# Vision tower on one core: the embedding in two halves, the selection ahead of the logits, and the last layers with new lags

## What is computed

```python
h = _L0_tok_ref(x, L0_tok_W, L0_tok_b)                   # patches 16x16 -> 256 features
h = _layernorm(h + _L0_attn_ref(h, ...))                 # 16 heads, q and k normed
h = _layernorm(h + _L0_ffn_ref(h, ...))                  # 8 experts, top 2, rms norm
h = _layernorm(h + _L1_attn_ref(h, ...))                 # delta rule, a scan over tokens
h = _layernorm(h + _L1_ffn_ref(h, ...))                  # receptance and key, relu squared
h = _layernorm(h + _L2_attn_ref(h, ...))                 # causal attention
h = _layernorm(h + _L2_ffn_ref(h, ...))                  # mixture of 64 small experts by argmax in groups of 16 tokens
h = _layernorm(h + _L3_attn_ref(h, ...))                 # s = lam*s + (1-lam)*x over the tokens
h = _layernorm(h + _L3_ffn_ref(h, ...))                  # int8 product with one scale for all tokens
```

```python
lam = sigmoid(x @ W + b)                                 # _L3_attn_ref
u_gated = (1.0 - lam) * x
s = lam_t * s + ug_t                                     # scan over the tokens of an image
x_int8 = clip(round(x2 / x_scale), -128, 127)            # _L3_ffn_ref, x_scale = max|x2| / 127
out = (x_int8 @ weight_int8.T) * x_scale * weight_scale.T + bias
```

## Time and profile before

| | us |
|---|---|
| median of 3 runs | 1481.62 (1480.22 to 1492.69) |
| profiled execution | 1482.68 |
| its span, first to last instruction | 1481.0 |
| PE busy | 1168.3 (79%) |
| DVE busy | 843.6 (57%) |
| ACT busy | 572.1 (39%) |
| POOL busy | 553.3 (37%) |

### The profile page before, as it was taken

The page is one execution under the profiler, slowest core; times in us unless marked ns, Lnnn a source line. Parts: engine busy times, 40 slices in busy tenths (PEclk is TensorE's granted clock), DMA queues, the critical chain, the costliest instruction groups (busy, mean ns, idle before and its releaser), DMA issues. The chain is left out here.

```text
span 1481.0 us, 23865 instructions
## 1 busy us (share of the span) xinstructions
PE 1168.3 (79%) x8627; PEld 853.3 (58%) x8627; DVE 843.6 (57%) x2014; ACT 572.1 (39%) x1356; POOL 553.3 (37%) x620
## 2 busy tenths in 40 slices
PE   4888886598999999676767777774899998686756
PEld 3666664487988989532334444342777776464432
DVE  2566565511212122556999999994577776324776
ACT  1444442111111211154566666661344444233436
POOL 0111111232332323333899999991112111011336
PEclk9999996699999999898898999995999999776565
DMA  3111100688888887386000000002000040055301
GB/s 128 32 38 44 44 9 15 231 331 334 306 314 303 320 304 265 103 214 163 0 0 1 1 1 1 1 1 78 8 12 8 12 172 2 1 214 183 113 15 58
DMA packets 83300, 162.18 MB, mean 110 GB/s; under 512 B 44080, under 2 KB 62128, under 8 KB 77168
## 3 DMA queue, kind: packets, MB, share of 16 engines
q1 hardware_dynamic: 55488, 111.23, 21.7%
q0 software_dynamic: 10512, 45.10, 8.3%
q10 hardware_dynamic: 17184, 4.33, 1.3%
HBM read 134.28 MB, written 26.35 MB: 108 GB/s over the span
## 5 line engine op out<-in xcount | busy, mean ns | idle before, releaser
L1398 PE MATMUL banks<-made,ident 128*128 128x512 f32 x256 | 152.4, 681 | 90.8 <-DVE made L1609 90.3
L895 PE MATMUL banks<-rowsT,w_up 128*128 128x128 f32 x1716 | 202.2, 278 | 0.1
L895 PEld LDWEIGHTS banks<-rowsT,w_up 128*128 128x128 f32 x1716 | 198.9, 195 | 0.7 <-DMA w_up<-in_up_w 0.4
L1661 POOL TENSOR_TENSOR ys<-xT_d,q_by_time 128x1024 f32<-128x1024 f32 x63 | 148.7, 2361 | 19.3 <-ACT xT_d L1481 9.8
L1504 ACT ACTIVATE banks<-banks,rate 128x256 f32<-128x256 f32 x256 | 104.1, 445 | 116.4 <-DVE made L1600 116.4
L1398 PEld LDWEIGHTS banks<-made,ident 128*128 128x128 f32 x256 | 41.7, 203 | 154.7 <-ACT banks L1504 129.9
L1665 POOL TENSOR_TENSOR ys<-ys 128x512 f32<-128x512 f32 x126 | 124.8, 990 | 9.9
L910 PE MATMUL banks<-w_down,hT 128*128 128x256 f32 x468 | 115.1, 388 | 0.6 <-DVE res L1079 0.6
L1069 DVE TENSOR_TENSOR hT<-banks,silu 64x128 f32<-64x128 f32 x39 | 11.0, 283 | 173.0 <-ACT silu L953 173.0
L839 POOL DMA_DIRECT2D w_down<-in_down_w x39 | 22.8, 584 | 197.6 <-PE banks L910 192.5
L910 PEld LDWEIGHTS banks<-w_down,hT 128*128 128x128 f32 x468 | 82.6, 189 | 22.0 <-issue 13.9
(11 more groups left out here) (315 smaller groups left out, 2388.4 us busy)
## 6 DMA issues: line engine op xcount, KB each, us to landing
w_up<-in_up_w SPq DMA_DIRECT2D x39, 1408.0 KB, 5.9
w_down<-in_down_w POOLq DMA_DIRECT2D x39, 768.0 KB, 4.9
inter<-res_x SPq DMA_DIRECT2D x16, 512.0 KB, 2.6
back<-inter SPq DMA_DIRECT2D x16, 512.0 KB, 3.7
patches<-in_patches SPq DMA_DIRECT2D x16, 384.0 KB, 3.1
f<-in_f SPq DMA_DIRECT2D x6, 1024.0 KB, 10.6
ys<-token_rows SPq DMA_DIRECT2D x16, 256.0 KB, 2.8
xn_rows<-xn_all SPq DMA_DIRECT2D x16, 128.0 KB, 1.7
```

The costliest lines, as they stand in the source:

```text
L895: ins = pe.matmul(out[:, m * P:(m + 1) * P], w[:, c, m * P:(m + 1) * P], x[:, c, :], start=(c == 0), stop=(c == 1))
L1398: pe.matmul(S[(t + 1) % 2][:, halves[h], :, :], ident[:, :], outer[:, halves[h], :, :], start=False, stop=True, skip_group_check=True).the ...
L1661: pool.tensor_tensor(qs[:, :, :, :], Sc[(t + 1) % 2][:, :, :, :], bcast(qt[:, t, :, :], 2, HD), ALU.mult).then_inc(sem("qs_made"), 1)
```

## The change

Embedding. `embed` is split: PE does `second_half(t)` at the start of a tick and `first_half(t+1)` after `values(t)`; `first_half(0)` comes before the loop. `turn_xn` moves on PE from behind `values` to behind `scores`, and waits for hT_copied too; `copy_xnT` moves on ACT from behind `copy_v` to behind `copy_hT`.

Middle layers. `select` (lag 5) comes ahead of `logit` (lag 4).

Last layers. mote_bias and own are loaded ahead of f1 and f2 on semaphores of their own; ACT and POOL wait for those alone at their start. The first tile's back is loaded in four pieces, two of them (12 of 16 quads) ahead of the last store. The scan is written with steps of x: y holds x(t-1) - x(t), made by POOL (`steps_of_x`), and state = (y + state) * lam gives s - x, so DVE adds 2x. xT, lam and y have a zero column ahead of each image in place of the memset. y is turned with four matmuls of 64 columns of weights each. All lags of the stage change. In the integer stage the clamp at -128 is gone (DVE writes qb in bf16 itself), the third norm goes from ACT (with POOL's shift) to POOL, `turn_v` has lag 2 and `int_sums` and `dequantize` lag 1; DVE's list (quantize lag 0, add_int lag 2) is as before.

```diff
-        def embed(t):
+        def embed(t, chunks):
+            for c in chunks:
+                ins = pe.matmul(X, patches[t % SLOTS_IN][:, c, :], w_tok[:, c, :], start=(c == 0),
+                                stop=(c == PC - 1), skip_group_check=True)
+            return ins
+
+        def first_half(t):
             pe.wait_ge(sem(f"patches{t % SLOTS_IN}"), 16 * (t // SLOTS_IN) + 16)
             if t >= 4:
                 pe.wait_ge(sem("xnT_copied"), t - 3)
-            for c in range(PC):
-                ins = pe.matmul(X, patches[t % SLOTS_IN][:, c, :], w_tok[:, c, :], start=(c == 0),
-                                stop=(c == PC - 1))
-            ins.then_inc(sem("embedded"), 1)
+            embed(t, range(0, PC // 2))
+
+        def next_half(t):
+            if t + 1 < T:
+                first_half(t + 1)
+
+        def second_half(t):
+            embed(t, range(PC // 2, PC)).then_inc(sem("embedded"), 1)
...
         def turn_xn(t):
             pe.wait_ge(sem("xn_made"), t + 1)
+            pe.wait_ge(sem("hT_copied"), min(t + 4, T))
             transposes(pe, halves(XNT), xn_all[:, t, :], ident[:, :], DC).then_inc(sem("xnT_made"), 1)
...
-        ticks([(0, embed), (2, turn_out), (0, turn_h), (2, project), (1, scores), (0, queries_keys), (0, values),
-               (3, turn_xn), (1, turn_p), (0, turn_qk), (3, route_scores), (1, attend)])
+        first_half(0)
+        ticks([(0, second_half), (2, turn_out), (0, turn_h), (2, project), (1, scores), (3, turn_xn),
+               (0, queries_keys), (0, values), (0, next_half), (1, turn_p), (0, turn_qk), (3, route_scores),
+               (1, attend)])
...
-        ticks([(2, copy_oT), (0, copy_hT), (0, squares), (1, exponent), (0, head_guess), (0, copy_v), (3, copy_xnT),
+        ticks([(2, copy_oT), (0, copy_hT), (3, copy_xnT), (0, squares), (1, exponent), (0, head_guess), (0, copy_v),
                (1, copy_PT), (0, copy_qk), (2, rms)])
...
         ticks([(1, turn_x1), (3, scores), (0, delta_out), (2, turn_x2), (1, receptance_key), (4, turn_x3),
-               (4, logit), (5, select), (3, turn_p), (1, key_value), (3, attend), (4, turn_perm),
+               (5, select), (4, logit), (3, turn_p), (1, key_value), (3, attend), (4, turn_perm),
...
-weights = [(mote_bias, "mote_bias"), (own, "own_tok"), (w_lam, "lam_w"), (b_lam, "lam_b"), (w8, "int8_w"),
-           (w_scale, "int8_scale"), (bias, "int8_b")]
+weights = [(w_lam, "lam_w"), (b_lam, "lam_b"), (w8, "int8_w"), (w_scale, "int8_scale"), (bias, "int8_b")]
+SPLIT = 12
...
+        sp.dma_start(mote_bias[:], io["mote_bias"]).then_inc(sem("mote_bias"), 16)
+        sp.dma_start(own[:], io["own_tok"]).then_inc(sem("own"), 16)
...
+        def first_back(quads):
+            for p in range(3):
+                sp.wait_ge(sem(f"stored{p}"), 16 * len(range(p, quads.stop, 3)))
+            at = slice(4 * quads.start, 4 * quads.stop)
+            for g in range(2):
+                sp.dma_start(back[0][g * ME + at.start:g * ME + at.stop, :, :], inter[0:GPT, at, :]
+                             .rearrange("(k g) e d -> g e k d", g=2)[g]).then_inc(sem("back0"), 16)
+
         for q in range(QUADS):
             sp.wait_ge(sem("res_low"), q + 1)
             sp.wait_ge(sem("res_high"), q + 1)
             sp.dma_start(inter[:, 4 * q:4 * q + 4, :], res[q % 3][:, :, :]).then_inc(sem(f"stored{q % 3}"), 16)
-        for p in range(3):
-            sp.wait_ge(sem(f"stored{p}"), 16 * len(range(p, QUADS, 3)))
-        for t in range(T):
+            if q == QUADS - 2:
+                first_back(range(0, SPLIT))
+        first_back(range(SPLIT, QUADS))
+        for t in range(1, T):
...
-            pe.wait_ge(sem(f"back{t % BACKS}"), 16 * (t // BACKS) + 16)
+            pe.wait_ge(sem(f"back{t % BACKS}"), 16 * (t // BACKS) + (64 if t % BACKS == 0 else 16))
...
-            transposes(pe, halves(scanned_bank(t)), y[t % 2], ident[:, :], DC).then_inc(sem("y_turned"), 1)
+            for c in range(DC):
+                for i in range(2):
+                    ins = pe.matmul(scanned_bank(t)[i * TOK:(i + 1) * TOK, c * P:(c + 1) * P],
+                                    y[t % 2][:, c, i, 1:TOK + 1], ident[:, :], start=True, stop=True,
+                                    skip_group_check=True)
+            ins.then_inc(sem("y_turned"), 1)
...
-        mix_back(0)
-        ticks([(2, turn_y), (0, turn_x), (0, one_ahead(mix_back)), (0, lam_logits)], 2)
+        ticks([(0, mix_back), (4, turn_y), (2, lam_logits), (1, turn_x)], 4)
         pe.wait_ge(sem("row_top"), 1)
         pe.transpose(banks[:, 2, 0:P], top[:, 0:1].to_broadcast([P, P]), ident[:, :]).then_inc(sem("tops"), 1)
         pe.wait_ge(sem("w_ready"), 1)
-        ticks([(0, turn_q), (1, turn_v), (0, int_sums)], 1)
+        ticks([(0, turn_q), (2, turn_v), (1, int_sums)], 2)
...
         def copy_xT(t):
             act.wait_ge(sem("xT_made"), t + 1)
             if t >= 2:
-                act.wait_ge(sem("ug"), t - 1)
-            act.copy(flat(xT[t % 2]), turned_bank(t)).then_inc(sem("xT_copied"), 1)
+                act.wait_ge(sem("stepped"), t - 1)
+                act.wait_ge(sem("lam_logits"), t - 1)
+            act.copy(segments(xT[t % 2])[:, :, 1:TOK + 1], spread(turned_bank(t))).then_inc(sem("xT_copied"), 1)
...
-        def third_norm(t):
-            if t >= 2:
-                act.wait_ge(sem(f"out{t % 2}"), 16 * (t // 2))
-            normed(3, res_q[t % 2][:, :], r3, t)
-
-        act.wait_ge(sem("weights"), 16 * len(weights))
+        act.wait_ge(sem("mote_bias"), 16)
...
+        act.wait_ge(sem("weights"), 16 * len(weights))
         act.copy(w[:, :, :], w8[:, :, :].bitcast(I8)).then_inc(sem("w_ready"), 1)
-        ticks([(0, first_norm), (0, copy_xT), (2, second_norm), (0, gate)], 2)
+        ticks([(1, first_norm), (2, gate), (1, copy_xT), (5, second_norm)], 5)
         act.wait_ge(sem("scaled"), 1)
-        ticks([(0, copy_qT), (0, dequantize), (2, third_norm)], 2)
+        ticks([(0, copy_qT), (1, dequantize)], 1)
...
+        def steps_of_x(t):
+            pool.wait_ge(sem("xT_copied"), t + 1)
             if t >= 2:
...
-        pool.wait_ge(sem("weights"), 16 * len(weights))
+                pool.wait_ge(sem("y_turned"), t - 1)
+            x_now = segments(xT[t % 2])
+            pool.tensor_tensor(segments(y[t % 2])[:, :, 1:TOK + 1], x_now[:, :, 0:TOK], x_now[:, :, 1:TOK + 1],
+                               ALU.subtract).then_inc(sem("stepped"), 1)
+
+        def third_norm(t):
+            root(3, t)
+            if t >= 2:
+                pool.wait_ge(sem(f"out{t % 2}"), 16 * (t // 2))
+            pool.tensor_scalar(res_q[t % 2][:, :], r3[t % 2][:, :], agg[3][t % 2][:, 0:1],
+                               agg[3][t % 2][:, 1:2], ALU.subtract, ALU.mult).then_inc(sem("ln3_done"), 1)
+
+        for b in (*xT, *lam, *y):
+            pool.memset(segments(b)[:, :, 0], 0.0).then_inc(sem("padded"), 1)
+        pool.wait_ge(sem("padded"), 6)
+        pool.wait_ge(sem("own"), 16)
         for t in range(T):
             pool.tensor_tensor(perm_t[:, t, :], perm_t[:, t, :], own[:, :], ALU.mult).then_inc(sem("owned"), 1)
-        ticks([(0, rstd(1)), (2, rstd(2))], 2)
-        ticks([(0, clamp), (2, rstd(3))], 2)
+        ticks([(0, rstd(1)), (1, steps_of_x), (4, rstd(2))], 4)
+        ticks([(0, third_norm)], 0)
 
...
-            dve.tensor_tensor(r2[t % 2][:, :], x[t % 4][:, :], scanned_bank(t), ALU.subtract
-                              ).then_inc(sem("added2"), 1)
+            dve.scalar_tensor_tensor(out=r2[t % 2][:, :], in0=x[t % 4][:, :], scalar=2.0, in1=scanned_bank(t),
+                                     op0=ALU.mult, op1=ALU.add).then_inc(sem("added2"), 1)
...
         def scan(t):
             dve.wait_ge(sem("lam"), t + 1)
-            dve.wait_ge(sem("xT_copied"), t + 1)
-            dve.scalar_tensor_tensor(out=flat(ug), in0=flat(lam[t % 2]), scalar=1.0, in1=flat(xT[t % 2]),
-                                     op0=ALU.subtract, op1=ALU.mult).then_inc(sem("ug"), 1)
-            dve.wait_ge(sem("ug"), t + 1)
-            dve.memset(flat(lam[t % 2]).rearrange("p (i t) -> p i t", t=TOK)[:, :, 0], 0.0
-                       ).then_inc(sem("cut"), 1)
-            dve.wait_ge(sem("cut"), t + 1)
-            if t >= 2:
-                dve.wait_ge(sem("y_turned"), t - 1)
-            dve.tensor_tensor_scan(y[t % 2][:, :], flat(lam[t % 2]), flat(ug), 0.0, ALU.mult, ALU.add
-                                   ).then_inc(sem("scanned"), 1)
+            dve.wait_ge(sem("stepped"), t + 1)
+            if t < 2:
+                dve.wait_ge(sem("padded"), 6)
+            line = y[t % 2][:, :, :, :].rearrange("p c i t -> p (c i t)")
+            dve.tensor_tensor_scan(line, line, lam[t % 2][:, :, :, :].rearrange("p c i t -> p (c i t)"), 0.0,
+                                   ALU.add, ALU.mult).then_inc(sem("scanned"), 1)
...
         def quantize(t):
             if t >= 2:
-                dve.wait_ge(sem("q_ready"), t - 1)
```

(7 more changed lines are left out.)

39 lines of the change are left out of this document (20 added, 19 removed).

## The result

| | before | after |
|---|---|---|
| median, us | 1480.92 | 1436.38 (1432.96 to 1438.29) |
| profiled execution, us | 1482.68 | 1434.60 |
| its span, us | 1481.0 | 1433.0 |
| mean granted clock of TensorE | 0.896 | 0.911 |

The ratio is 0.968, with an interval of 0.9635 to 0.9726: a gain of 41 to 54 us, 44.5 by the medians. The forecast said 36.6 (1481.6 to 1445) and a range down to 1436. The direction was right, and the gain is larger than forecast. 1436.38 lies at the very edge of the range; by the ratio, which sets aside that the kernel before was 0.7 us faster in these runs than in the forecast's, it is 0.968 x 1481.62 = 1434.2, outside it.

What follows compares the result with a forecast made beforehand. No single engine was taken as the bound; each stage was read by its steady tick. Terms 15.5 + 2.6 + 6.5 + 1.0 + 18.2 - 6.0 = 37.8 us off 1482.7 gave 1444.9, said as 1445; range 1436 to 1460.

Steps and rivals of the forecast that it cites:

- The scan stage: Last layers' scans: less VectorE work and new lags cut the tick from 4.87 to 3.65 us; 18.2 us gained, bounds 12.2 to 20.5.
- The embedding: Embedding with first attention: half an embedding fills a TensorE stop, tick 1.0 us shorter over fifteen tiles; 15.5 us gained.
- The middle layers: Selection ahead of logits: 4.6 us gained over twelve ticks, a loss at the tail; net 2.6 us, bounds -2 and 4.6.
- The experts: Last layers' experts: early mote_bias and own remove TensorE's 6.07 us stop, 6.5 us; first way back loaded partly early, 1.0 us.
- The integer stage: Last layers' integer product: VectorE waits behind its quantizing for both turns, tick 2.79 us against 2.26; 6.0 us lost.
- (a): Scan stage: GpSimd's step of x and VectorE's scan collide on the SBUF ports, 9.9 us less gain, 1455; chance 0.10.
- (b): Scan stage hardly gains, since some wait holds the old 4.87 us tick: 1463; chance 0.07.
- (c): Embedding: TensorE's stop only moves elsewhere: 1461; chance 0.06.
- (e): Scan stage: GpSimd's wait for the turn of y closes an 8.3 us loop each tick, slower than before: 1515; chance 0.03.
- (d): Integer stage does not stall, TensorE finishing both turns before VectorE: 2.5 us gained instead of 6.0 lost, 1436; chance 0.12.

Runs made afterwards that it cites:

- a variant with TensorE busy 66% of the time: The changed kernel with the scan stage's old lags, GpSimd's steps of x and the scan on them kept: 1454.95 us, the stage 75.6 us.

## Why the forecast was off, point by point

**The scan stage (18.2 said, 26.1 measured) is the step that failed, as a size.** The mechanism is as it was put: a chain with TensorE at half clock before, VectorE after. The sum was 15 x 3.65 + 13.7. Measured it is 15 x 3.33 + 10.7.

- The tick, 0.32 us too long, 4.8 us in all. I took 0.13 of it for a clock that would come and go; it stayed at 1.00 from 1335 to 1365. The other 0.19 is VectorE's work. I had 3.75 less 0.43, 3.32 us a tile, and 0.2 us of gaps. In the steady window below VectorE is busy 28.12 of 30 us, 3.12 us of a tick, and idle 0.21: the gaps were right. The durations of a tile's instructions, added up, fell by 0.48 us (3.94 to 3.46); the rest is that more of them overlap, which the old lags did not give (3.33 us busy a tile there).
- What lies beside the ticks, 3.0 us. I said that one tile's way through stays at 13.7 us. It went up, to 15.6 (10.1 from the first mixing to the first scan at 1329.91, 5.5 from the last scan at 1374.89 to the end), but the ticks at both ends, where not all steps of VectorE run, are short once VectorE sets the tick: the first scans are 1.93 and 3.13 us apart and the last ones 2.12, 2.40 and 2.11, together 5.0 us under five full ticks. In the variant with the old lags, bound by a chain, all scans lie 4.03 to 4.48 us apart, at the ends too.

```profile
1340.00:1370.00 30.00, 22.27 (x229) 15.30 (x228) 28.12 (x91) 17.93 (x46) 22.90 (x46) 1.00 0.33 105
```

(The changed kernel.) The lower bound of my own term, a tick of 3.5 us at full clock, was itself too high: it took the busy time of a stage with waits for the work of a stage without them.

**The embedding (15.5 said, 18.5 measured)** is the second miss. The fifteen ticks came out at 15.5. I left out the first tick, ahead of the first turn of the probabilities, where half an embedding went into a stop too: 2.5 us. The earlier start, 0.58 us, is chance.

**The middle layers (2.6 said, 2.9 measured)** fit by luck, by opposite errors: 6.3 us in the ticks where I said 4.6, and a tail that costs 3.4 to 6 us where I said 2.

**The experts (7.5 said, 7.3 measured)** likewise: about 8 for the early bias and -1.1 for the early way back, where I said 6.5 and +1.0. I had named SP's two more issues ahead of the last store and priced them too low, and had put the store's later landing and the cut in two pieces at nothing.

**The integer stage (6.0 lost, 6.3 measured)** was right in place, row and size, and the one term that pointed to a repair.

**The rivals.** (a) The ports: one scan of sixteen grew, by 0.11 us, and one of GpSimd's two roots by 0.33 us in each steady tick; neither cost the tick anything. (b), (c) and (e) did not happen; GpSimd's loop never filled, and even 0.61 us more left the tick as it was. (d) had the right whole time (1436) for the wrong reason: the stall is there. The range was cut too close at the fast end, because I added the bounds of all terms as if only one could be at its end, and let the largest term's bound rest on an estimate.

## What to carry to other kernels

When a stage changes from a chain to an engine that is always busy, take the new tick from that engine's busy time less everything removed, and expect the first and last ticks to shrink with it. In a tick, let no engine wait for a step that another engine has queued behind a step which waits for the first: turning v before q, or adding a tick later, was worth 7 to 10 us here. Before a transfer is cut to start part of it early, count what the pieces put ahead of the last store. Price an order in the last ticks apart from the steady ones, and judge an edit by its stage when the unchanged stages vary more than it can give.

## What the runs showed of the hardware that I had not expected

TensorE's granted clock came and went in one code. In one execution the old scan stage had scans 4.91 us apart at half clock and then 3.93 and 5.91 in turn as the clock rose and fell. The kernel before spent the first 52 us of that stage at 0.50, and a variant with TensorE busy 66% of the time held 1.00. Unchanged layers took 755.8 to 763.5 us with a clock of 0.93 to 0.92. The Trainium skill's page "TensorE: Matmul & The Clock Gate", section "Part 1: The HAM clock gate (the "warmup" mystery)", says that the clock follows how busy TensorE has been; these runs show its two levels, and by their busy shares alone I couldn't have told which level a stage would have.

GpSimd's work on a single column, which takes 0.27 us, takes 0.70 beside a scan of VectorE, and ends 0.06 us after it. A scan that starts inside GpSimd's step of x waits in its turn: 0.81 and up to 0.94 us in place of 0.70.

One transfer of 512 KB cut in two took 5.04 us to the first matmul that reads it, uncut 3.91.
